# Attention worked in pairs of chunks, with every inverse root as one GpSimd power

## What is computed

```python
q = split_heads(layernorm(x) @ Wq) * scale          # 16 heads of 64
k, v = split_heads(ctx @ Wkv)                       # 128 context tokens of width 512
k = concat(null_key, k); v = concat(null_value, v)  # 129 keys
out = softmax(q @ k.T) @ v
out = layernorm_affine(out @ Wout)                  # rsqrt(var + 1e-6)
x = x + tanh(g_xattn) * out
x = x + tanh(g_ffn) * ffn(layernorm(x))             # global maxima set the quantization scales
```

## Time and profile before

| | us |
|---|---|
| median of three runs (lowest to highest) | 581.29 (580.51 to 581.66) |
| the profiled execution | 581.69 |
| its span, first to last instruction | 579.6 |

### The profile page before, as it was taken

The page is one execution under the profiler, slowest core; times in us unless marked ns, Lnnn a source line. Parts: engine busy times, 40 slices in busy tenths (PEclk is TensorE's granted clock), DMA queues, the critical chain, the costliest instruction groups (busy, mean ns, idle before and its releaser), DMA issues. The chain is left out here.

```text
span 579.6 us, 10953 instructions
## 1 busy us (share of the span) xinstructions
PE 529.9 (91%) x3936; PEld 458.1 (79%) x3936; DVE 408.3 (70%) x1051; ACT 311.9 (54%) x878; POOL 123.5 (21%) x129
## 2 busy tenths in 40 slices
PE   2999999999999999999999999998779999807898
PEld 2877889888888988898898888887467878604797
DVE  4679844855674675476458457848686888999996
ACT  2734633543444263354336326525668659988992
POOL 3001310230130132023113102312303118930000
PEclk9999999999999999999999999999999999957899
DMA  7932001100110110020011001002201000000033
GB/s 255 357 116 74 1 1 54 40 2 1 54 36 0 54 36 0 0 90 0 0 54 36 0 1 38 1 2 93 73 18 33 5 2 0 6 32 0 2 95 124
DMA packets 18478, 25.86 MB, mean 45 GB/s; under 512 B 1216, under 2 KB 15808, under 8 KB 18448
## 3 DMA queue, kind: packets, MB, share of 16 engines
q1 hardware_dynamic: 18192, 25.17, 13.2%
q0 software_dynamic: 256, 0.30, 0.3%
HBM read 21.27 MB, written 4.19 MB: 44 GB/s over the span
## 5 line engine op out<-in xcount | busy, mean ns | idle before, releaser
L843 ACT ACTIVATE probs<-bank,nmax 128x129 f32<-128x129 f32 x256 | 90.9, 368 | 123.0 <-DVE nmax L1205 123.0
L1637 POOL TENSOR_TENSOR probs<-probs,rinv 128x512 f32<-128x512 f32 x64 | 66.7, 1043 | 333.2 <-DVE rinv L1213 333.2
L615 PE MATMUL bank<-wv,ctxT 128*128 128x512 f32 x384 | 94.5, 398 | 0.0
L607 PE MATMUL bank<-ctxT,wk 128*128 128x256 f32 x672 | 88.9, 282 | 0.1
L607 PEld LDWEIGHTS bank<-ctxT,wk 128*128 128x128 f32 x672 | 83.6, 188 | 0.3 <-DVE ctxT L1072 0.3
L615 PEld LDWEIGHTS bank<-wv,ctxT 128*128 128x128 f32 x384 | 70.4, 188 | 16.9 <-issue 1.2
L851 ACT ACTIVATE oT<-bank,ncol 128x256 fp32r<-128x256 f32 x64 | 30.6, 478 | 52.9 <-PE bank L679 52.8
L1217 DVE COPY pT<-bank 128x512 f32<-128x512 f32 x64 | 43.5, 680 | 18.0 <-PE bank L669 17.6
L607 PE MATMUL bank<-xnT,wq 128*128 128x256 f32 x336 | 54.7, 298 | 1.0 <-DVE v L1132 1.0
L843 ACT ACTIVATION_READ_ACCUMULATOR probs<-bank,nmax 128x1 f32 x256 | 51.9, 203 | 0.0
L607 PEld LDWEIGHTS bank<-xnT,wq 128*128 128x128 f32 x336 | 43.1, 188 | 8.3 <-issue 1.2
(11 more groups left out here) (170 smaller groups left out, 831.3 us busy)
## 6 DMA issues: line engine op xcount, KB each, us to landing
craw<-in_ctx SPq DMA_DIRECT2D x8, 512.0 KB, 3.5
stage<-in_L_xattn_Wkv SPq DMA_DIRECT2D x8, 512.0 KB, 12.1
xa<-in_x SPq DMA_DIRECT2D x8, 256.0 KB, 2.8
xr<-in_x SPq DMA_DIRECT2D x8, 256.0 KB, 2.9
x_scratch<-y SPq DMA_DIRECT2D x7, 256.0 KB, 2.2
x2all<-x_scratch SPq DMA_DIRECT2D x1, 1792.0 KB, 8.5
xres<-x_scratch SPq DMA_DIRECT2D x6, 256.0 KB, 2.9
out<-yout SPq DMA_DIRECT2D x6, 256.0 KB, 2.2
```

The lines of the kernel that those rows point to most:

```text
L607: last = mm(bk[:, n * TG:(n + 1) * TG], wt[a][:, k, f], act_t[b][:, k, :], start=(k == 0 and i == 0), stop=(k == kk - 1 and i == len(TERMS ...
L615: last = mm(bk[:, :], ctxT[a][:, k, b * S:(b + 1) * S], wv[w][:, k, h * 512:(h + 1) * 512], start=(k == 0 and i == 0), stop=(k == KC - 1 a ...
L843: last = nc.scalar.activation(probs[:, c % 2, u, 0:NK], score_bank[c % 2][h][:, b * QW:b * QW + NK], ACT.Exp, bias=nmax[:, c % 2, u:u + 1] ...
L1637: G.tensor_tensor(probs[:, c % 2, :, 0:S], probs[:, c % 2, :, 0:S], rinv[:, c % 2, :].rearrange("p (u o) -> p u o", o=1).to_broadcast([P, ...
```

## The change

Attention goes by pairs p of chunks, four a group. `scores` makes eight products of 128 columns into two full banks, one for each half h of the array; the null key is no column any more. Instead the null key is subtracted from every key when Q is split (`keys`, so a Q unit is split in two ACT instructions), the null key's score becomes zero, the maxima are cut at zero by a small DVE instruction, and its exponential is a fifth small ACT instruction of a pair's half (`null_exp`), added to the row sum before the reciprocal. Exponentials, sums, POOL's multiplies, transposes and copies go by halves of a pair (h = 0, 1). The transposes of half 0 are written into the score bank that the exponentials have read. The values of a pair fill one bank, and `out_high` and `out_low` take 512 columns at once.

DVE puts both maxima of the next pair first in a slot, then the one chain that is dealt to the slot (`beside`: the attention norm, the statistics or the normalisation of tokens, or a step of the FFN weights), the splits, the two copies and the two sums. `x2_statistics` and `x2_range` of the group before move to the end of the group, in the last group behind F8. One Q unit moves from group 6 to group 7. W waits for the low parts pair by pair.

All inverse roots become one POOL instruction, a power with exponent -0.5 (`root`), and DVE only adds epsilon; DVE's Newton steps and ACT's Sqrt with its table load go. The residual stream of groups 0 to 5 is loaded back ahead of the last group's transfers, that of group 6 behind them.

```diff
-    PLAN = ([["Q0"], ["Q1"], ["Q2"], ["Q3"], ["Q4"], ["Q5", "V00"], ["Q6", "V10"], ["Q7", "X"]],
...
+    PLAN = ([(["Q0", "Q1"], ["Q2"]), (["Q3", "Q4", "Q5"], []), (["Q6", "Q7"], []), (["V00", "V10", "X"], [])], [],
             ["V01", "V11", "C", "W"])
...
+    PLAN_PENULT = ([(["Q0"], ["Q1"]), (["Q2", "Q3"], []), (["Q4", "Q5"], []), (["V00", "V10"], [])], [], ["W"])
+    PLAN_FINAL = ([(["Q6"], ["Q7"]), ([], ["V01"]), (["V11"], []), (["F0", "F1"], [])], ["F2", "F3", "F4"],
+                  ["F5", "F6", "F7", "F8", "W"])
...
-                        if b == 0:
-                            wait(pe, ot_lo, g * NS + NS)
                         for k in range(KF):
+                            if b == 0 and k % 2 == 0 and k >= KF - 4:
+                                pe.wait_ge(ot_lo, g * NP + k // 2 + 1)
...
+            def scores(g, p):
...
+                wait(pe, pt_copied, 2 * (g * NP + p) - 3)
+                for u in range(4):
+                    c, b = 2 * p + u // GB, u % GB
                     for h in range(2):
                         rows = slice(h * DH, (h + 1) * DH)
-                        last = mm(score_bank[c % 2][h][:, b * QW:b * QW + QW], qk[rows, c, b, 0:S],
-                                  qk[rows, c, GB + b, 0:QW], start=True, stop=True)
+                        last = mm(score_bank[p % 2][h][:, u * S:(u + 1) * S], qk[rows, c, b, :],
+                                  qk[rows, c, GB + b, :], start=True, stop=True)
                 last.then_inc(scores_done, 1)
...
+            def prob_transposes(g, p, h):
+                n = 2 * (g * NP + p) + h
+                pe.wait_ge(norm_done, n + 1)
+                if h == 1:
+                    wait(pe, pt_copied, n - 1)
+                pt = transposed(p, h)
                 for u in range(4):
-                    last = nc.tensor.transpose(pt_bank[:, u * P:(u + 1) * P], probs[:, c % 2, u, 0:S], ident[:, :])
+                    last = nc.tensor.transpose(pt[:, u * P:(u + 1) * P], probs[:, p % 2, h, u, :], ident[:, :])
                 last.then_inc(pt_done, 1)
...
+                        last = mm(value_bank(p)[rows, u * S:(u + 1) * S], v[:, b, c, rows], pT[:, p % 2, h, u, :],
+                                  start=True, stop=True)
                 last.then_inc(pv_done, 1)
...
+                for p in range(NP):
+                    if p + 1 < NP:
+                        scores(g, p + 1)
+                    ahead, behind = slots[p]
+                    run(ahead)
+                    for h in range(2):
+                        prob_transposes(g, p, h)
+                    if p:
+                        values(g, p - 1)
+                    run(behind)
+                if not (isinstance(g, int) and g == NG - 1):
                     scores(g + 1, 0)
...
+                run(mid)
+                values(g, NP - 1)
+                run(tail)
...
+            def keys(dst, src):
+                return nc.scalar.activation(dst, src, ACT.Identity, bias=nk_neg[:, 0:1])
...
+                    high(qk[:, c, 0:GB, :], bk[:, 0:TG].rearrange("p (b s) -> p b s", s=S))
+                    keys(qk[:, c, GB:2 * GB, :],
+                         bk[:, TG:2 * TG].rearrange("p (b s) -> p b s", s=S)).then_inc(unit_hi, 1)
...
+            def exps(g, p, h):
+                act.wait_ge(max_done, 2 * (g * NP + p) + h + 1)
+                wait(act, pt_done, 2 * (g * NP + p) - 2)
...
+                for p in range(NP):
+                    ahead, behind = slots[p]
+                    if not final:
+                        run(ahead[:1])
+                    if p + 1 < NP:
+                        exps(g, p + 1, 0)
+                    run(ahead[:1] if final else ahead[1:2])
+                    if p + 1 < NP:
+                        exps(g, p + 1, 1)
+                    run(ahead[1:] if final else ahead[2:])
+                    if p:
+                        out_high(g, p - 1)
+                    run(behind)
                 if not final:
-                    exps(g + 1, 0)
-                out_high(g, NS - 1)
-                for u in tail:
-                    if u == "C":
...
-            def root(k):
-                act.wait_ge(root_in, k + 1)
-                if k in (0, 3):
-                    cols = slice(0, known) if k == 0 else slice(known, NT)
-                    var, out_root = rs3[:, 1, cols], rs3[:, 2, cols]
-                else:
-                    var, out_root = rs[:, 5, k - 1:k], rs[:, 6, k - 1:k]
-                nc.scalar.activation(out_root, var, ACT.Sqrt).then_inc(root_out, 1)
...
-            def newton(link, r):
-                link(V.scalar_tensor_tensor(out=r[2], in0=r[0], scalar=-0.5, in1=r[0], op0=ALU.mult, op1=ALU.mult))
-                link(V.tensor_tensor(r[2], r[2], r[1], ALU.mult))
-                link(V.scalar_tensor_tensor(out=r[0], in0=r[2], scalar=1.5, in1=r[0], op0=ALU.add, op1=ALU.mult))
...
+                ln1.count(V.tensor_scalar(rs[:, 1, :], mv[:, 0:2, 1], EPS_LN, None, ALU.add))
                 ln1.end()
...
+            def ln_apply(n):
+                dve.wait_ge(ln1_root, n + 1)
...
+                ln2.count(V.tensor_scalar(rs[:, 5, :], mv[:, 2:4, 1], EPS_OUT, None, ALU.add))
+                ln2.end()
             def attention_norm(g, dst):
-                rsqrt_end(ln2.link, [rs[:, 4 + i, :] for i in range(3)])
-                ln2.end()
+                dve.wait_ge(ln2_root, g + 1)
...
+            def maxima(g, p, h):
+                n = 2 * (g * NP + p) + h + 1
+                if h == 0:
+                    dve.wait_ge(scores_done, g * NP + p + 1)
+                V.tensor_reduce(nmax[:, p % 2, h, :], score_bank[p % 2][h][:, :].rearrange("p (u s) -> p u s", s=S),
+                                AX.X, ALU.max, negate=True).then_inc(keys_max, 1)
+                dve.wait_ge(keys_max, n)
+                V.tensor_scalar(nmax[:, p % 2, h, :], nmax[:, p % 2, h, :], 0.0, None, ALU.min).then_inc(max_done, 1)
+            def inverse_sums(g, p, h):
+                n = 2 * (g * NP + p) + h + 1
+                dve.wait_ge(exp_done, n)
+                V.tensor_tensor(rowsum[:, p % 2, h, :], rowsum[:, p % 2, h, :], null_exp[:, p % 2, h, :],
+                                ALU.add).then_inc(total_done, 1)
+                dve.wait_ge(total_done, n)
+                V.reciprocal(rinv[:, p % 2, h, :], rowsum[:, p % 2, h, :]).then_inc(rinv_done, 1)
+            def prob_copy(g, p, h):
+                dve.wait_ge(pt_done, 2 * (g * NP + p) + h + 1)
+                V.tensor_copy(pT[:, p % 2, h, :, :],
+                              transposed(p, h)[:, :].rearrange("p (u s) -> p u s", u=4)).then_inc(pt_copied, 1)
...
+            def to_root(var, dst, eps):
+                V.tensor_scalar(dst, var, eps, None, ALU.add).then_inc(root_in, 1)
...
+                        if u == "F8":
+                            x2_statistics(g - 1, y[:, :, :])
+                            dve.wait_ge(x2_stats, 2 * (NG - 1) - 1)
+                            to_root(mean_var[:, 0:known, 1], rs3[:, 1, 0:known], EPS_LN)
+                            x2_range(g - 1, y[:, :, :])
+                            dve.wait_ge(root_out, 1)
...
+                    if p == (0 if final else 1) and not first:
+                        attention_norm(g - 1, y)
+                    if p == 1 and feeds(g):
+                        ln_stats(g + 2)
+                    if p == 2 and feeds(g):
+                        ln_apply(g + 2)
+                    if first and p == 0:
...
+                for p in range(NP):
+                    ahead, behind = slots[p]
+                    if p + 1 < NP:
+                        for h in range(2):
+                            maxima(g, p + 1, h)
+                    if not final:
+                        beside(p)
+                    run(ahead)
+                    for h in range(2):
+                        prob_copy(g, p, h)
+                    if p + 1 < NP:
+                        for h in range(2):
+                            inverse_sums(g, p + 1, h)
+                    if p:
+                        out_low(g, p - 1)
+                    if final:
+                        beside(p)
+                    run(behind)
                 if not final:
...
+                if not final:
+                    inverse_sums(g + 1, 0, 0)
+                run(tail[:1])
+                if not final:
+                    inverse_sums(g + 1, 0, 1)
+                run(tail[1:])
+                if first:
+                    weight_values(1)
+                    weight_scales(2)
+                elif not final:
+                    x2_statistics(g - 1, y[:, :, :])
+                    x2_range(g - 1, y[:, :, :])
                 if not final:
                     attention_stats(g, y)
...
             settle()
             dve.wait_ge(x2_stats, 2 * (NG - 1))
-            r = root_columns(slice(known, NT))
-            root_start(mean_var[:, known:, 1], r, EPS_LN)
```

(34 more changed lines are left out.)

357 lines of the change are left out of this document (136 added, 221 removed).

## The result

The changed kernel takes 563.65 us (median of 4 runs, 563.08 to 564.34) where the kernel before took 580.90 beside it (580.26 to 581.66): a ratio of 0.970, 95% interval 0.9685 to 0.9716. It is faster, by 17.3 us; the forecast was 562.0 in a range of 557 to 574. The profiled execution took 564.34.

What follows compares the result with a forecast made beforehand. PE's own instruction stream was taken to bound looped groups, the attention chain the last group. Savings of 1.5 (start) + 5 x 2.20 (loop) + 3.8 and 2.2 (groups 6, 7) + 1.2 (roots) = 19.7 us gave 562, range 557 to 574.

Steps and rivals of the forecast that it cites:

- The second rival: PE's blocks: a doubled block costs twice the old one, 10 us less saved, 572 us; chance 0.06.
- the fifth: PE's seams only turn into waits for the same banks and nothing moves, 581 us; chance 0.02.
- the 9.1 us from scores to probabilities: Looped groups: second half's probabilities ready 9.1 us after pair's scores; PE's transposes due 15.1, 14 and 12.4 in slots 0-2.
- The first rival: A pair's chain is too long and PE waits 0.35 us in each of 28 slots: 572 us; chance 0.18.
- margin of 0.7: Score bank: free 1.3 us after its transposes start, behind one copy, and wanted by the next scores at 1.99.
- DVE has 20 spare: Looped group: added clamps, sums and reciprocals cost DVE under 4 us, returned by dropped Newton chains, with 20 us spare.
- Saved 1.5: First group: V00's split 2.45 us later, but the group takes 47.34 plus 0.6 and ends at 96.3 instead of 97.78.
- the walk: Group 7, step by step from its first scores: W starts after 31.4 us instead of 33.62, 2.2 less.
- the term of 1.2: Roots at the end: dropped reciprocals and Newton steps gain 1.2 us, between -0.4 and 2.3.
- with at most 14 numbers a partition: Price of GpSimd's power: near its small 128x128 select, taken as 0.4 us and hidden by DVE's 0.48 pass.
- The third rival: Slow power, waited for four times at the end: at 3 us each, 570 us; chance 0.10, of which 0.05 slower.
- The fourth: Only the first power is late, by its code load, and holds the first X: 564 us; chance 0.04.

Runs made afterwards that it cites:

- The two transposes: Kernel after with one more full-array transpose a pair, inside the score block (575.78 us) or, as control, among the second half's transposes (566.60 us).
- late_copies: Kernel after with VectorE's sums and reciprocals of the next pair ahead of the copies of this pair's transposed probabilities: 571.51 us.
- a part of the pairs: Kernel after with the old roots instead of powers, VectorE's looped Newton chains placed where the kernel before had them: 567.07 us.
- late_maxima: Kernel after with VectorE's work beside in each slot ahead of the next pair's two maxima: 564.08 us.
- start_early: Kernel after with first pair's sums and reciprocals behind V00's split, weights' scales behind V11's, second group's root ahead of GpSimd's first normalisation: 561.62 us.
- The run with the seam: Kernel after with one more full-array transpose in the middle of each pair's score block: 575.78 us.
- the run with the powers alone: Kernel before with every inverse root by a power on GpSimd, chunks as they were: 580.72 us against 581.07.
- the early end: Kernel after with the end's 14-column root split: 12 columns at the end of group 6, two asked for behind F8: 562.88 us.

## Why the prediction came out as it did

**PE's blocks.** Right, to a tenth: scores 1.09 (predicted 1.09), values 1.02 (1.02), period 47.31 (47.34), no idle time. The two transposes show what an excursion costs: four fewer a group at 0.34 make 1.36 of the 2.23 that a looped group gained. The rest, the starts of blocks of values among half-array work, agrees with the prices that were read from the rows, but no run tests it alone. The second rival (a doubled block costs twice, 1.30) and the fifth (seams turn into waits) are out.

**The chain.** The 9.1 us from scores to probabilities hold in slot 0: from the end of the scores at 193.04 to the end of the second multiply at 202.1 it is 9.05. That two of its terms cancel is luck: the exponentials end 6.8 us after the scores, not 7.6, and the second sum takes 0.88 instead of 0.2 (the last section shows beside what). In slot 1 it is 10.8, since both reciprocals stand behind the copies, which wait for the transposes; due after 14.0, so hidden all the same. The first rival did not come. Its margin of 0.7 was right: in slot 1 the transposes start at 208.12, the first copy ends at 209.4 and the scores start at 210.11. What was wrong is the expectation of the run with late copies, which let the scores wait for both copies where the prediction had one. That the copies go first is worth 7 to 8 us (7.9 in the medians, 7.1 between the traces), most of it in group 6. That the maxima go first is worth nothing that could be measured.

**The cover of the chains.** "DVE has 20 spare" was right as a sum over a group and says nothing of a place. Two chains of eleven steps, one put ahead of V00's split and one ahead of two copies, cost 5.2 us in the first group alone, 1.5 of it through the clock, with the same 20 to spare; a few instructions further back they cost 0.3. The prediction had no term for it because the change takes these chains away. It also means that the gain doesn't quite split into a part of the pairs and one of the powers: by the traces from the first scores on, 15.6 and 1.8 make 17.4, not 18.4. (In the medians 13.6 and 0.35 make 14, not 17, but there the start is in the sums.)

**Start.** "Saved 1.5" brought 0.46. What I had costed was right: from the first scores of group 0 to those of pair 1 it lost 1.92 (predicted 2.1, the lateness of V00's split), and from there to the first scores behind W it took 48.06 (predicted 47.94), so the group by itself gained 1.48 (64.93 to 63.45). But the first scores themselves came at 33.87 instead of 32.85, and for that stretch I had no term. ScalarE's first copy of the k weights and PE's k units, before and then after, split this 1.0:

```profile
14.05 1.06 ACT L827 ACTIVATE wk<-stage 128x1024 fp32r<-128x1024 f32 x1 [3.22 <-DMA stage<-in_L_xattn_Wkv]
...
21.28 11.63 PE L594 MATMUL bank<-ctxT,wk 128*128 128x256 f32 x96 [0.62 <-DVE wk L1072]
```

```profile
14.42 1.06 ACT L853 ACTIVATE wk<-stage 128x1024 fp32r<-128x1024 f32 x1 [5.14 <-DMA stage<-in_L_xattn_Wkv]
...
22.13 11.81 PE L607 MATMUL bank<-ctxT,wk 128*128 128x256 f32 x96
```

The copy waits for the weights' transfer and starts 0.37 later. In nine of the thirteen traces the k units start 7.2 us behind that copy, and PE waits for VectorE's part of the k weights, as in the second line. In the other four (the kernel after, late_copies, late_maxima, start_early) the clock fell to half behind PE's wait for q0's split; there PE waits for no weights but comes late itself, 7.7 to 8.0 us behind the copy: 0.48 more in the kernel after. The k units then take 0.17 longer to the first scores. Neither part is shown to belong to the change: eight kernels have the same instructions up to there, and in these eight traces the copy starts between 13.60 and 15.00, and the clock fell in four and not in the other four. The run with the seam waited 1.7 us at the same place and kept its clock. Why the clock falls in one execution and not in another stays open.

**Groups 6 and 7.** Group 6 took 38.23 (37.9), with the predicted 0.9 of W's wait for the low part (0.93 measured). Group 7 followed the walk: transposes of pairs 1 to 3 end 9.1, 18.0 and 22.2 after its first scores (9.6, 18.5, 22.7), W starts at 31.37 (31.4).

**Roots.** The mechanism was right and the size off: the term of 1.2 brought 0.26. The prices say how. From the statistics of W's first half to VectorE's last maximum it was 9.30 before (424.04 to 433.34) and is 7.56 (408.21 to 415.77): 1.74 gained, two single roots at 0.44 each and the last root wholly hidden. Against it the statistics start 1.48 later behind W, because two things meet: the first power has fourteen columns and takes 2.60, not 0.4, and group 6's statistics, moved ahead of its request, put that request 1.3 later, a step that the prediction named without a price. Each by itself costs next to nothing. In the run with the powers alone VectorE waits 1.54 for the same power, but nothing was moved, and the statistics start 3.43 behind W (424.96 against 421.53); in the early end the statistics are moved, but the power has two columns, and it is 3.21 (405.47 against 402.26). I had priced all powers by the smallest instruction of GpSimd, "with at most 14 numbers a partition"; but the time goes with the columns, (2.60 - 0.55) / 13 = 0.16 each. The early end takes back exactly this 1.5.

**The slow power and its first call.** The third rival needed 3 us in four powers in a row; one of four had 2.6. (At 7 us its own terms, four times what exceeds 1.1, give 586 and not 588.) The fourth did not come: the first power, at 5.90, took 0.75, where all but one of the others of its shape take 0.70, and it started as soon as GpSimd had issued its own transfers (5.89). The 6 us that the Trainium skill (GPSIMD Engine Reference, Instruction dispatch) gives for the first call of a freshly loaded kernel are not seen here, in any of the traces with powers.

## What to carry to other kernels

Where PE is full, look inside the full stretch: put the starts of a few blocks side by side, and count how often the stream goes from one array mode to another. Here each excursion costs 0.34 us, and fewer, longer blocks in one mode were worth more than any wait that could be removed.

Spare time of an engine is a statement about a sum. Before a chain is put on an engine with time to spare, or taken from it, ask what stands behind it in that queue and who waits for that; the same chains cost 5.2 us or 0.3 in the first group. And to test one half of a change alone, put what is restored where the old kernel had it, or the run measures the place.

An unknown instruction is priced at the size that it will have on the critical path, not at the smallest.

## What was not expected of the hardware

GpSimd's power takes time by columns: 0.55 us for 1, 0.70 for 2, 2.28 for 12, 2.60 for 14 (the early end ran the twelve), about 0.16 a column on top of 0.4, while a multiply of 512 columns takes 1.04.

GpSimd and VectorE can hold each other up, with no wait in the rows. VectorE's sum of a pair's second half and GpSimd's multiply of the first half, in a looped group of the kernel after:

```profile
199.88 0.88 DVE L1223 TENSOR_TENSOR rowsum<-rowsum,null_exp 128x4 f32<-128x4 f32 x1 [0.26 <-ACT null_exp L886]
```

```profile
199.70 1.04 POOL L1665 TENSOR_TENSOR probs<-probs,rinv 128x512 f32<-128x512 f32 x1 [4.74 <-DVE rinv L1226]
```

By itself the sum takes 0.13 to 0.17 us. One that starts so early inside a multiply that it could end before it ends 0.01 to 0.02 us behind it instead, every time in this trace, here at 200.76 against 200.74. It goes the other way too: in all nine traces of pairs with powers, the third two-column power starts 0.2 us into a VectorE pass over 128x1536 (1.75 us) and takes 2.13 instead of 0.70, to 0.55 behind the end of the pass. In the run with the powers alone no such pass stands beside it, and it takes 0.69. In the looped groups PE waits for neither.

One full-array transpose costs 0.115 us among others and 0.46 between half-array products. The granted clock can fall to half for some 3 us (0.50 from 20 to 22 us in the kernel after), behind a wait of PE, here 2.1 us long; in the run with the early end, which has the same instructions there, PE waited 1.1 us and the clock stayed at 1.00 throughout the start.
